# Attention heads: row maxima turned in one matmul, exponentials in nine equal pieces, and two engines' orders changed

## The reference, cut to what matters

```
z = q @ k.T            # causal, 1024 x 1024 for each of 32 heads
p = exp(0.25 * (z - rowmax(z)))  where z is one of the row's 128 largest, else 0
out = (p @ v) / p.sum()
```

## Time and profile before

| what | value |
|---|---|
| median of 3 executions | 3160.02 us (3157.77 to 3161.55) |
| profiled execution, its own time | 3160.4 us |
| its span (first to last instruction) | 3158.6 us |
| heads stage in the span | about 2066 to 3044 us |

### The profile page before, as it was taken

The page is one execution under the profiler, slowest core; times in us unless marked ns, Lnnn a source line. Parts: engine busy times, 40 slices in busy tenths (PEclk is TensorE's granted clock), DMA queues, the critical chain, the costliest instruction groups (busy, mean ns, idle before and its releaser), DMA issues. The chain is left out here.

```text
span 3158.6 us, 50984 instructions
## 1 busy us (share of the span) xinstructions
PE 2873.4 (91%) x16015; PEld 1719.3 (54%) x16153; DVE 2456.8 (78%) x4628; ACT 1975.7 (63%) x4218; POOL 1650.8 (52%) x3659
## 2 busy tenths in 40 slices
PE   8899999999999999999999989837888888888889
PEld 4455455455454464454554544515666666666654
DVE  6678687697696796786876977848988998989846
ACT  2464554554554554545545533469999999999923
POOL 3236245254264263362462544767777777777613
PEclk9999999999999999999999999958999999999989
DMA  2222122232232132231221220000000000000000
GB/s 91 66 79 95 67 97 84 73 107 67 73 121 86 60 109 80 70 111 67 85 89 67 96 80 1 28 24 1 2 2 2 2 2 2 2 2 2 2 28 27
DMA packets 65805, 169.65 MB, mean 54 GB/s; under 512 B 11776, under 2 KB 19328, under 8 KB 64512
## 3 DMA queue, kind: packets, MB, share of 16 engines
q1 hardware_dynamic: 53872, 114.12, 11.1%
q10 hardware_dynamic: 11664, 52.24, 4.7%
HBM read 161.08 MB, written 5.24 MB: 53 GB/s over the span
## 5 line engine op out<-in xcount | busy, mean ns | idle before, releaser
L2100 ACT ACTIVATE X<-ah_z,ah_trial 128x256 bf16<-128x256 f32 (+6 forms) x896 | 738.4, 836 | 31.3 <-POOL ah_trial L2207 19.8
L1199 ACT ACTIVATE m_mix<-m_mix,m_cs 128x128 f32<-128x128 f32 x1024 | 312.8, 388 | 254.2 <-DMA m_mix<-cs_rows 254.1
L2030 PE MATMUL ah_ps_o<-a_v,X 128*128 128x17 f32 x2304 | 308.5, 260 | 0.0
L2030 PEld LDWEIGHTS ah_ps_o<-a_v,X 128*128 128x128 f32 x2304 | 291.7, 194 | 0.0
L1081 POOL TENSOR_TENSOR m_xdec<-m_xdt,m_decay_out 128x512 f32<-128x512 f32 x112 | 142.3, 1270 | 213.1 <-DVE m_xdt L1325 202.1
L1109 POOL TENSOR_TENSOR m_squares<-m_squares 128x256 f32<-128x256 f32 x128 | 106.1, 829 | 276.2 <-ACT m_squares L1211 276.2
L1005 PE MATMUL m_ps_d<-m_w_out,m_gate 128*128 128x512 f32 x512 | 235.2, 602 | 0.0
L1005 PE MATMUL m_ps_x<-m_w_out,m_gate 128*128 128x512 f32 x512 | 233.6, 599 | 0.0
L2277 DVE TENSOR_SCALAR_CACHE_REDUCE X<-ah_z,ah_cut 128x256 bf16<-128x256 f32 (+6 forms) x224 | 193.6, 875 | 44.2 <-POOL ah_cut L2212 44.2
L2111 ACT ACTIVATE X<-ah_ps_e 128x512 f32<-128x512 f32 (+3 forms) x384 | 188.2, 491 | 25.3 <-PE ah_ps_e L2017 16.3
L2298 DVE MAX8 ah_top<-ah_ps_m 128x8 f32<-128x384 f32 (+6 forms) x215 | 176.9, 823 | 26.1 <-PE ah_ps_m L1980 25.4
(11 more groups left out here) (330 smaller groups left out, 7557.9 us busy)
## 6 DMA issues: line engine op xcount, KB each, us to landing
m_mix<-cs_rows SPq DMA_DIRECT2D x128, 512.0 KB, 4.3
m_w_proj<-in_w_proj ACTq DMA_DIRECT2D x69, 512.0 KB, 3.3
m_fade<-fade_rows SPq DMA_DIRECT2D x224, 128.0 KB, 3.0
m_w_out<-in_w_out ACTq DMA_DIRECT2D x7, 2048.0 KB, 7.7
X<-in_x SPq DMA_DIRECT2D x8, 256.0 KB, 4.6
m_w_out<-in_w_out SPq DMA_DIRECT2D x1, 2048.0 KB, 9.9
x_away<-X SPq DMA_DIRECT2D x1, 2048.0 KB, 7.3
out<-X SPq DMA_DIRECT2D x8, 256.0 KB, 2.0
```

The source lines that it names most:

```text
L1199: act.activation(mix[:, u % 3, h, :], mix[:, u % 3, h, :], ACT.Relu, bias=cs[:, c, h0 + h:h0 + h + 1], scale=-1.0).then_inc(lag_done, 1)
L2030: last = pe.matmul(ps_o[:, t, :], eT[:, g % 3, b * P:(b + 1) * P], v[:, b0 + b, h // REP, :], start=i == 0 and b == 0, stop=b0 + b == t, s ...
L2100: act.activation(sign[:, at % 2, 0:(t + 1) * P], z[:, h % RING, cols(t)], ACT.Sign, bias=trial[:, h % RING, 0, t - 1:t], scale=-1.0, accum ...
```

## The change

Four things are done at once. (1) The row maxima: instead of eight matmuls that put each tile's parts in a row of their own (4 used rows of 128) and two copies of 128x512 into `rows`, one matmul turns all 32 columns of parts (4 for each of 8 tiles) and one copy of 128x128 brings them to `rows[:, h % 2]`. The stationary operand of the rows' matmul in `exponents` is now one of eight, `minus_rows[:, t]`, with its values on tile t's four rows. They are made in the set-up from `own_rows`, a constant of 128x8, by one more DMA and eight operations of DVE; one full memset and two small ones go, a larger one shrinks. (2) The pieces: the 36 blocks are cut into nine pieces of exactly four, across tiles where need be; the lists that place them are new. (3) POOL: `split_max` stands after the first move of a round and `first_cut` after the second. (4) DVE: `divide` stands after the first two takes. PE turns the maxima after tile 4, ACT copies them before the last sweep (`ROWS_BEFORE = 3 * W`, the 22nd count).

```diff
-    CHUNKS = [(t, b) for t in range(NT) for b in range(0, t + 1, 4)]
+    BLOCKS = [(t, b) for t in range(NT) for b in range(t + 1)]
+    CHUNKS = [BLOCKS[i:i + 4] for i in range(0, len(BLOCKS), 4)]
...
-    CHUNKS_AFTER_MARKED = ((), (), (), (), (), (7,), (9,), ())
-    CHUNKS_AFTER_SCORES = ((), (2,), (3, 4), (5,), (6,), (8,), (10,), (11,))
-    LAST_BUT_ONE = ((), (2, 3), (4, 5, 6), (7, 8, 9, 10, 11), (), (), (), ())
-    LAST_CHUNKS = ((), (), (), (), (0, 1), (2, 3), (4, 5), (6, 7))
+    CHUNKS_AFTER_MARKED = ((), (), (), (), (), (5,), (7,), (8,))
+    CHUNKS_AFTER_SCORES = ((), (), (2,), (3,), (4,), (6,), (), ())
+    LAST_BUT_ONE = ((), (2,), (3, 4, 5), (6, 7, 8), (), (), (), ())
+    LAST_CHUNKS = ((), (), (), (), (0,), (1,), (2,), (3,))
...
-    ROWS_BEFORE = {14: 0, len(SWEEPS) * W: 1}
+    ROWS_BEFORE = 3 * W
...
-        SET_UP = 11
+        SET_UP = 16
...
+            sp.dma_start(own_rows[:], env.dram["own_rows"]).then_inc(table_in, 16)
...
-                for t in range(4):
-                    last = pe.matmul(ps_x[:, t * P:(t + 1) * P], parts[:, 4 * half + t, :], env.ident_bf[:],
-                                     start=t == 0, stop=True, skip_group_check=True)
-                last.then_inc(row_done, 1)
+                pe.matmul(ps_x[:, 0:P], all_parts, env.ident_bf[:], start=True, stop=True,
+                          skip_group_check=True).then_inc(row_done, 1)
...
-                    if live(n - 2) and t in (2, 7):
-                        turned_rows(n - 2, t // 7)
+                    if live(n - 2) and t == 4:
+                        turned_rows(n - 2)
...
-                act.activation(eT[:, g % 3, 0:w * P], ps_e[g % 2][:, 0:w, :].rearrange("p b q -> p (b q)"), ACT.Exp,
+                act.activation(eT[:, g % 3], ps_e[g % 2][:].rearrange("p b q -> p (b q)"), ACT.Exp,
...
-                act.activation(rows[:, half * BANK:(half + 1) * BANK], ps_x[:], ACT.Copy).then_inc(rows_done, 1)
+                act.activation(rows[:, h % 2], ps_x[:, 0:P], ACT.Copy).then_inc(rows_done, 1)
...
-                if live(n - 2):
-                    split_max(n - 2)
-                if live(n + 1):
-                    first_cut(n + 1)
-                for back, k in sweeps_of(n):
+                for i, (back, k) in enumerate(sweeps_of(n)):
                     if live(n - back):
                         move(n - back, k)
+                    if i == 0 and live(n - 2):
+                        split_max(n - 2)
+                    if i == 1 and live(n + 1):
+                        first_cut(n + 1)
...
+            for t in range(NT):
+                dve.tensor_scalar(minus_rows[:, t], env.ones, own_rows[:, t:t + 1], None, ALU.mult).then_inc(set_up, 1)
             dve.wait_ge(set_up, SET_UP)
...
-                if live(n - 4):
-                    divide(n - 4)
                 if live(n - 2):
                     take(n - 2, 1)
                     take(n - 2, 2)
+                if live(n - 4):
+                    divide(n - 4)
```

More of the change, by code:

```diff
@@ L1856, in attention_heads_fast @@
         row_rest = sb("row_rest", [P, NT])
-        rows = sb("rows", [P, S], BF16)
+        rows = sb("rows", [P, 2, P], BF16)
         trial = sb("trial", [P, RING, 2, W])
@@ L1882, in attention_heads_fast @@
         sign = spare[:, 5 * BANK:7 * BANK].bitcast(BF16).rearrange("p (r c) -> p r c", r=2)
[L1883 removed]
+        all_parts = spare[:, 7 * BANK:7 * BANK + P // 2].bitcast(BF16)
+        parts = all_parts[:, 0:4 * NT].rearrange("p (t q) -> p t q", t=NT)
         ps_z = ctx.enter_context(nc.psum_tensor("ah_ps_z", [P, S], F32))
@@ L1996, in exponents @@
             def exponents(h, i):
-                t, b0 = CHUNKS[i]
-                w = min(4, t + 1 - b0)
                 g = h * NCH + i
+                out = ps_e[g % 2]
                 if g >= 2:
                     pe.wait_ge(exp_done, g - 1)
[L2003 to L2014, removed]
+                pe.wait_ge(rows_done, h + 1)
+                if CHUNKS[i][-1][0]:
+                    pe.wait_ge(pick_done, h * W + CHUNKS[i][-1][0])
@@ new lines, in exponents @@
+                clear = True
+                for t in range(CHUNKS[i][0][0], CHUNKS[i][-1][0] + 1):
+                    mine = [j for j, (u, _) in enumerate(CHUNKS[i]) if u == t]
+                    lo, w = mine[0], len(mine)
+                    if t:
+                        for j in mine:
+                            at = OFF[t] + CHUNKS[i][j][1] * P
+                            pe.matmul(out[:, j, :], picked[:, h % 2, at:at + P], ident_back[:], start=clear, stop=False,
+                                      skip_group_check=True)
+                            clear = False
+                    pe.matmul(out[:, lo:lo + w, :], minus_rows[:, t], rows[:, h % 2].unsqueeze(1).to_broadcast([P, w, P]),
+                              start=clear, stop=False, skip_group_check=True)
+                    clear = False
@@ L2015, in exponents @@
+                for j, (t, b) in enumerate(CHUNKS[i]):
+                    last = pe.matmul(out[:, j, :], kT[:, h // REP, b * P:(b + 1) * P], qT[:, h, t * P:(t + 1) * P],
                                      start=False, stop=True, skip_group_check=True)
-                if b0 + w == t + 1:
-                    last = pe.matmul(out[:, w - 1, :], env.future_bf[:], env.ident_bf[:], start=False, stop=True,
-                                     skip_group_check=True)
+                    if b == t:
+                        last = pe.matmul(out[:, j, :], env.future_bf[:], env.ident_bf[:], start=False, stop=True,
+                                         skip_group_check=True)
@@ L2028, in add_v @@
                     pe.wait_ge(divided, h)
-                for b in range(w):
-                    last = pe.matmul(ps_o[:, t, :], eT[:, g % 3, b * P:(b + 1) * P], v[:, b0 + b, h // REP, :],
-                                     start=i == 0 and b == 0, stop=b0 + b == t, skip_group_check=True)
+                for j, (t, b) in enumerate(CHUNKS[i]):
+                    last = pe.matmul(ps_o[:, t, :], eT[:, g % 3, j * P:(j + 1) * P], v[:, b, h // REP, :],
+                                     start=i == 0 and j == 0, stop=b == t, skip_group_check=True)
                 last.then_inc(av_done, 1)
@@ L2079, in _ @@
                 turn_and_add(h - 1, LAST_BUT_ONE[t])
-                if t in (4, 5):
-                    turned_rows(h, t - 4)
+                if t == 4:
+                    turned_rows(h)
                 turn_and_add(h, LAST_CHUNKS[t])
-            turn_and_add(h, range(8, NCH))
+            turn_and_add(h, range(4, NCH))
             add_v(AH * NCH - 2)
@@ L2128, in _ @@
                                 exponential(g)
-                        if live(n - 2) and at in ROWS_BEFORE:
-                            row_out(n - 2, ROWS_BEFORE[at])
+                        if live(n - 2) and at == ROWS_BEFORE:
+                            row_out(n - 2)
                         if live(n - back):
@@ L2350, in _ @@
             h = AH - 1
-            divide(h - 2)
             take(h, 1)
             take(h, 2)
+            divide(h - 2)
             for t in range(1, NT):
@@ L2437, in constants @@
                           np.broadcast_to(width + 2.0 * (TOPK - AIM), n.shape), np.full(n.shape, -1.0)], 1)
+    own_rows = np.where(k[:, :1] // 4 == np.arange(NT)[None, :], np.where(k[:, :1] % 4 == 3, -1024.0, -1.0), 0.0)
     inv_freq = (np.float32(1) / np.float32(THETA) ** (np.arange(0, AD, 2, dtype=np.float32) / np.float32(AD)))
```

49 lines of the change are left out of this document (20 added, 29 removed).

## The result

The changed kernel takes 3199.49 us (median of four executions, 3181.31 to 3207.51); the kernel before, run beside it on the same chip, 3160.78 us (3157.77 to 3165.79). The ratio is 1.0108, with a 95% interval of 1.0089 to 1.0127: 1.1% slower, where 1.1% faster was forecast and 3143 us was the upper end of the range. The profiled execution is the fastest of the four, 3181.31 us with a span of 3179.5. What it shows is thus the mild case.

The account below looks back on a forecast made before the run. The prediction took ACT as the bound, with DVE next. 29 rounds going from 28.49 to 27.5 us give 28.7, less 2.1 for set-up, plus 6.5 and 2.2: 35.3 us off 3160.4, so 3125 us, range 3112 to 3143.

Parts of the forecast that it names:

- The mechanism of ACT: ACT's round: 0.95 us less for pieces and copy, 0.28 less waiting for POOL's trial, so 28.49 becomes 27.26 us.
- the 0.80 of the copy: On ACT, two copies of 512 columns become one of 128, saving 0.80 us a round.
- 0.15: On ACT, nine pieces instead of twelve save three fixed costs of 0.05 us, 0.15 us a round.
- POOL and DVE: POOL's final cut comes 0.1 to 0.2 us later against ACT; DVE's chain stays at 27.2 us, its product wait goes.
- Rival (a): The chain of DVE and PE becomes the bound: 28.0 us a round, 3139.6 us in all; chance 0.24.
- The step that failed is PE's: PE has about 0.2 us less work a round, nothing on the path; only when the pieces are ready counts.
- five in 26 rounds: Rounds with a MAX8 wait of over 1 us in their middle, costing ACT 0.25 us a round on average.
- 1.31 us: DVE's longest MAX8 wait, at a low granted clock, taken as the most that one such disturbance costs.
- some 5 to 10 us: Sign: ACT's waits on PE's pieces in the heads stage, where they were under 3 us.
- Rival (c): Slower by TensorE's clock: PE rests longer and falls to 1.2 GHz; 3185 us at two falls a round; chance 0.06.
- 28.72: Break-even round: the present 28.49 us plus 0.23 from start and end, passed at 1.3 falls a round.
- Start and end: Outside the bound rounds: set-up loses 2.1 us, the first three rounds gain 6.5, the last head gains 2.2.

Follow-up runs that it names:

- e4: The changed kernel with useless matmuls on PE ahead of the marking of tile 4 (six) and of tile 7 (five): 3132.6 us.
- e3: The kernel before with the new row maxima only, old pieces and old orders: 3161.7 us, ratio 1.0001 to the kernel before.
- e15: e4 with the old orders of POOL and DVE: 3164.4 us.
- e16: The changed kernel with the twelve old pieces and six useless matmuls ahead of the marking of tile 4: 3151.7 us.
- e5: The changed kernel with six useless matmuls ahead of the marking of tile 4 alone: 3132.8 us.
- e9: The changed kernel with two more useless matmuls in each of the two places of `stay_awake`: 3199.1 us.
- e12: The kernel before without its seven useless `stay_awake` matmuls a round: 3210.7 us, ratio 1.0164 to the kernel before.
- e7: The kernel before with its twelve pieces moved to places like those of the nine: 3171.3 us.
- e13: e4 with twelve more useless matmuls ahead of the last head's first marking: 3120.6 us.
- e6: The changed kernel with five useless matmuls ahead of the marking of tile 7 alone: 3144.0 us.
- e10: The kernel before with the new orders of POOL and DVE only, old maxima and pieces: 3421.7 us, ratio 1.0828 to the kernel before.
- e11: The changed kernel with three useless matmuls instead of six ahead of the marking of tile 4, none ahead of tile 7: 3137.0 us.
- e8: The changed kernel with six useless matmuls ahead of tile 4's marking and the last piece moved ahead of tile 7's marking: 3130.0 us.

## Why the prediction was wrong

**The mechanism of ACT was right.** The pitches hold. The timeline of ACT in a clean round of the changed kernel, against the earlier trace rows (the round of 27.40 us between the cuts at 2945.9 and 2973.3):

```profile
2959.75 0.62 ACT L2114 ACTIVATE X<-ah_ps_e 128x512 f32<-128x512 f32 x1
2960.23 1.19 ACT L2105 ACTIVATE X<-ah_z,ah_trial 128x1024 bf16<-128x1024 f32 x1
...
2961.36 0.30 ACT L2122 ACTIVATE ah_rows<-ah_ps_x 128x128 bf16<-128x128 f32 x1
2961.52 0.55 ACT L2105 ACTIVATE X<-ah_z,ah_trial 128x256 bf16<-128x256 f32 x1
```

0.48 and 0.16 us as priced. The sum 28.49 - 0.95 - 0.28 = 27.26 us meets 27.24 (e4's usual round); with what disturbs it 27.32, where 27.5 was forecast. What the parts do, one by one, is another matter: the 0.80 of the copy turned into a wait for the trial until the orders moved it (e3, e15), and the pieces gave 0.55, not 0.15, because ACT's wait for a piece went with them (e16).

**POOL and DVE were right.** In a clean round POOL's second move, first cut and third move start as laid out:

```profile
2954.92 0.21 POOL L2177 TENSOR_TENSOR ah_trial<-ah_signs,ah_table 128x7 f32<-128x7 f32 x1 [1.11 <-ACT X L2105]
...
2959.90 0.20 POOL L2152 TENSOR_TENSOR ah_guess<-ah_stats,ah_table 128x7 f32<-128x7 f32 x1
2963.61 0.20 POOL L2177 TENSOR_TENSOR ah_trial<-ah_signs,ah_table 128x7 f32<-128x7 f32 x1
```

A move of 5.0 us, a first cut of 3.7. DVE's wait on `ps_o` went and nothing came in its place. Rival (a) did not occur: with the clock held DVE is busy 94% and ACT does not wait for it.

**The step that failed is PE's.** "About 4 x 0.055 = 0.2 us less ...: nothing on the path. What counts is when the pieces are ready." I asked when PE's work would be ready and never where PE would rest. The work that left the places ahead of its two waits for the picks was counted as a saving of nothing. What the runs showed in its place: the rest ahead of tile 4 grew from 1.1 to 2.2 us, that ahead of tile 7 to 1.7, the clock fell 23 times in 25 rounds instead of 7, and filling the rest ahead of tile 4 took all falls and some 60 us away (e4, e5). A warning stood in the trace of before: falls at rests of 1.6 us idle at most, by the prediction's own reading in one round of five; that `stay_awake` was kept was no protection, since its work stands elsewhere (e9), while before it was just enough (e12).

**Two sizes went with it.** I took the number of falls as given, five in 26 rounds (the clock's own record shows 7 in 25); it became 23 in 25. And I priced a fall at 1.31 us, from one MAX8. Measured, (29.48 - 27.32) x 25 / 23 = 2.35 us each, from nothing to 8 us a round, for in a stretch of 10 to 17 us at half speed PE is the bound (in the longest round it was busy 94%). Both enter as a product: 23 x 2.35 = 54 us, where 5 x 1.31 = 6.6 had been set. ACT's waits on PE's pieces, "some 5 to 10 us", became 48.6 for the same reason.

**Rival (c) is what happened,** at a chance of 0.06. Its mechanism was right, its point of decision (1.3 falls a round) too high by the price: at 2.35 us a fall on clean rounds of 27.3 its 28.72 are passed at (28.72 - 27.3) / 2.35 = 0.6 falls a round, and 0.92 came. What spoke against it in my text, "falls come in one round of five", was a property of the old order of work, which the change undid. The Trainium skill's page "TensorE: Matmul & The Clock Gate" (section "HAM oscillation — how this bites in real kernels") tells of such repeated falls from idle gaps; this trace agrees, with 23 of them and 154 us at 1.2 GHz. The page's example has waits of about 3 to 5 us for DMAs; here the rests are of 1.7 to 2.2 us and for another engine.

**Start and end.** DVE's first start is at 2068.48 us, not 2071; but over the kernels with the same set-up it lies between 2067.8 and 2075.0, so a term of 2.1 us can't be read from one. The third cut comes 2.9 us earlier than before (2182.6 to 2179.7) in the changed kernel and 7.2 in e4 (2175.4), against 6.5 - 2.1 = 4.4: of the right size. From the last cut to the last divide it takes 36.5 us instead of 38.5: 2.0, near the 2.2 forecast, but that is luck, since over all the profiles this stretch lies between 33.8 (e3) and 54.0 us (e7, e12). The difference of the two spans adds up: -2.9 to the third cut, +25.2 in the 29 rounds, -2.0 in the last head, +0.6 behind it, 20.9 us.

With the clock held in the rounds the forecast would have been off by 8 us (3132.6 against 3125). The last head's low clock can account for that: e4's profile has it and the changed kernel's mostly not (45.9 us from last cut to last divide against 36.5). With the rest there filled, e13 comes to 3120.6, inside the range.

**What stays open.** Why in e13 a second fall comes late in the last head, and in which executions. What besides its length decides whether a rest brings a fall is not settled either: e5 bears one rest of 1.7 us a round, e6 mostly bears one of 2.2, the changed kernel does not bear both, though they lie 12 us apart, and e12 does not bear two of 1.4 close together. These counts are from one profiled execution each. The nine pieces were not tried with the old maxima and orders. The new maxima were not tried apart from the orders with the clock held in a kernel of nine pieces, since the orders stall without them (e10).

## What to carry to other kernels

When a change takes work from an engine that is not the bound, look where in the engine's order the work stood: if it stood ahead of a wait, the rest there grows, and two rests a round that had grown were enough here to halve TensorE's clock and make it the bound; price that by how many rounds already show a low clock and by what the bound would be at half speed, not by the shortest disturbance seen. Filling the longest rest (six useless matmuls, 1.3 us a round) gave over 60 us back here; the same kind of work elsewhere (0.86 us a round) gave nothing. And parts of a change can be worth nothing singly (the maxima) or cost 8% (the orders) and gain 1.2 us a round together, so undo them one at a time with the disturbance held off.

## What the runs showed of the hardware that was not expected

- TensorE's granted clock fell to half 23 times in 25 rounds although the engine was busy 88% of the time and no rest was over 2.3 us. With 0.65 us of the 2.2 filled it fell twice, with 1.3 us filled never, in one profiled execution each (e11, e5).
- Removing seven useless matmuls (1.5 us of a round of 28.4) from the kernel before cost 50 us (e12).
- A low stretch was 3.4 us long in the kernel before, each of the seven times, and up to 17 us in the changed one; up to 41 us were seen in the last head (e8), where TensorE was busy nearly without a pause.
